# Gated delta net on one NeuronCore: beta moves into the decay scan, key products are multiplied straight from PSUM, query tables take one factor

## What is computed

```python
beta  = sigmoid(x @ W_b.T)                        # per token and value head (32 heads)
decay = exp(-softplus(x @ W_a.T + dt_bias) * exp(A_log))
kk    = kk / max(norm(kk), 1e-12)                 # 16 key heads of 128, 2 value heads for each
def step(state, inp):
    q_t, k_t, v_t, b_t, d_t = inp
    delta = (v_t - k_t . state) * b_t
    state = state * d_t + outer(k_t, delta)
    return state, q_t . state
out = rmsnorm(o) * silu(z);  y = out @ W_out.T
```

## Time and profile before

| | |
|---|---|
| median of 3 runs | 4566.03 us (4562.16 to 4568.08) |
| the profiled execution | 4563.68 us, its span 4561.9 us |
| the 64 sections | from about 135 us to 3100 us of the span |
| PE busy over the span | 88%, VectorE 69%, ACT 49%, POOL 42% |
| granted TensorE clock, mean | 0.957 (1.00 from 500 us to 3000 us) |

### The profile page before, as it was taken

One profiled execution on the slowest core, in us unless ns is written; L12 is line 12 of the kernel. 1 busy time (PEld: TensorE's weight loads), 2 busy tenths in 40 slices (PEclk: granted clock), 3 DMA queues, 4 the chain that ended last, 5 costly groups with the idle time before them and its releaser, 6 DMA issues. The chain is left out here.

```text
span 4561.9 us, 75168 instructions
## 1 busy us (share of the span) xinstructions
PE 4014.6 (88%) x26288; PEld 2924.0 (64%) x26288; DVE 3163.8 (69%) x5082; ACT 2239.2 (49%) x4061; POOL 1893.7 (42%) x1852
## 2 busy tenths in 40 slices
PE   3899999999999999999999999985788879389998
PEld 2677777677777776777767677762344444168887
DVE  3788888888888888888888888874555556532222
ACT  1565656565655556565656565652444445321111
POOL 1364545554554546454555455542233332411110
PEclk8899999999999999999999999996899989689999
DMA  2001010101010101101010101103444553000001
GB/s 74 15 29 35 27 34 20 41 24 32 30 36 25 36 20 32 33 26 35 20 41 24 32 29 34 26 15 69 78 84 77 85 83 59 38 23 19 19 14 37
DMA packets 134066, 172.39 MB, mean 38 GB/s; under 512 B 12524, under 2 KB 79980, under 8 KB 133132
## 3 DMA queue, kind: packets, MB, share of 16 engines
q1 hardware_dynamic: 131212, 166.03, 15.5%
q10 hardware_dynamic: 2432, 1.05, 0.1%
HBM read 143.12 MB, written 21.76 MB: 36 GB/s over the span
## 5 line engine op out<-in xcount | busy, mean ns | idle before, releaser
L405 PE MATMUL pj<-xh,w_hi 128*128 128x512 f32 x1536 | 686.4, 447 | 25.4 <-ACT conv_k L612 16.7
L990 POOL TENSOR_TENSOR silu_z<-silu_z,exp_z 128x512 f32<-128x512 f32 x128 | 184.6, 1442 | 1212.7 <-ACT exp_z L629 1212.7
L405 PE MATMUL pj<-xh,w_lo 128*128 128x512 f32 x1536 | 607.5, 395 | 0.0
L405 PE MATMUL pj<-xl,w_hi 128*128 128x512 f32 x1536 | 602.9, 392 | 0.0
L1510 DVE TENSOR_REDUCE row_max<-s 128x1 f32<-128x512 f32 x512 | 342.0, 685 | 264.4 <-PE s L1264 260.7
L975 POOL TENSOR_SCALAR b_t<-qk_masked,beta_section 128x256 f32<-128x256 f32 (+1 forms) x512 | 490.7, 967 | 20.2 <-ACT qk_masked L714 19.6
L1444 ACT ACTIVATE probs<-s 128x512 f32<-128x512 f32 x512 | 290.6, 595 | 335.8 <-PE s L1288 267.5
L756 DVE SCALAR_TENSOR_TENSOR conv_v<-conv_in,conv_w_section,conv_v 128x512 f32<-128x512 f32 x384 | 402.0, 1047 | 19.4 <-ACT conv_v L612 5.5
L680 ACT ACTIVATE kk_masked<-tp 128x512 f16<-128x512 f32 x320 | 191.3, 598 | 321.8 <-PE tp L496 318.2
L405 PEld LDWEIGHTS pj<-xh,w_hi 128*128 128x128 f32 x1536 | 291.9, 190 | 81.0 <-issue 28.9
L405 PEld LDWEIGHTS pj<-xh,w_lo 128*128 128x128 f32 x1536 | 289.7, 189 | 67.3
(11 more groups left out here) (259 smaller groups left out, 10258.9 us busy)
## 6 DMA issues: line engine op xcount, KB each, us to landing
w_raw<-in_w_in SPq DMA_DIRECT2D x128, 256.0 KB, 3.4
decays<-decay_by_head SPq DMA_DIRECT2D x64, 512.0 KB, 3.8
decays<-decay_by_head SPq DMA_DIRECT2D x64, 256.0 KB, 4.9
q_stack<-qk_parts SPq DMA_DIRECT2D x128, 128.0 KB
k_stack<-qk_parts SPq DMA_DIRECT2D x128, 128.0 KB
f_raw<-in_f_w SPq DMA_DIRECT2D x32, 256.0 KB, 2.6
x_all<-in_x SPq DMA_DIRECT2D x4, 1024.0 KB, 11.2
source<-in_ctx SPq DMA_DIRECT2D x8, 512.0 KB
```

The lines of the kernel that those rows point to most:

```text
L405: mm = pe.matmul(pj[j % 2][:, :], a[:, j, k * P:(k + 1) * P], b[:, k, bp * WIN:(bp + 1) * WIN], start=(n == 0), stop=(n == 3 * KT - 1))
```

## The change

1. `scan_diag` goes. Its place in the scan takes `beta_diag`, a tile of 128 x 4 x 386 with beta of the token on the diagonal, so that the cumulated products come out of the scan already times beta. POOL makes it for the next section (`pool_beta`, two TENSOR_TENSOR of 4 x 128 columns each from the identity and `beta`), behind `pool_b`; `beta_s`, its VectorE copy (L737), goes.
2. `a_t` is made from the PSUM bank of the key product and `decays` (one factor, no copy of the keys by ACT): four instructions of two heads each, in the tail of the section before (`dve_a(t, b, c)`), instead of eight at the section's start.
3. `b_t` is the query product times `decays`: two TENSOR_TENSOR of 4 x 256 and 4 x 128 columns, instead of sixteen instructions. ACT copies only the two query products (`act_queries`).
4. PE makes both key products first (they no longer wait for the query convolution), ahead of the second chunk's first product, and the two query products later. The two projection halves that stood there move down by one place each; the gate's second projection ends one place later.
5. `kk_masked`, whose storage `u_i[0]` and `t_i[0]` used, becomes `t_and_u0`, a tile of its own. Waits follow.

The core of the diff:

```diff
-            dve.tensor_tensor_scan(dec[:, i, :], dec[:, i, :], diag, 0.0, ALU.mult, ALU.add).then_inc(E["dec"].sem, 1)
-        def dve_a(dve, s):
-            E["km"].wait(dve, s, 3)
-            E["beta_s"].wait(dve, s, 0)
-            for q in range(NM):
-                E["dec"].wait(dve, s, q)
-                for c, sl in enumerate((slice(0, SEQ), slice(SEQ, TRI))):
-                    before = dec[:, slot(q), sl.start + c:sl.stop + c]
-                    dve.scalar_tensor_tensor(out=a_t[:, q, sl], in0=kk[:, q // PV, sl],
-                                             scalar=beta_s[:, 2 * (q // PV) + c, q % PV:q % PV + 1], in1=before,
-                                             op0=ALU.mult, op1=ALU.mult).then_inc(E["at"].sem, 1)
-            E["at"].wait(dve, s, 7)
+            dve.tensor_tensor_scan(dec[:, i, :], dec[:, i, :], beta_diag[:, i, :], 0.0, ALU.mult, ALU.add).then_inc(E["dec"].sem, 1)
+        def dve_a(dve, t, b, c):
+            E["kq"].wait(dve, t, b)
+            E["dec"].wait(dve, t, b * PV + PV - 1)
+            sl = (slice(0, SEQ), slice(SEQ, TRI))[c]
+            by_head = dec[:, b:NM:2, sl.start + c:sl.stop + c]
+            dve.tensor_tensor(a_t[:, b * PV:(b + 1) * PV, sl], by_head,
+                              kq_bank[b][:, sl].unsqueeze(1).to_broadcast([P, PV, sl.stop - sl.start]), ALU.mult)\
+               .then_inc(E["at"].sem, 1)
+        def dve_inverse(dve, s):
+            E["at"].wait(dve, s, 3)
...
             E["delta"].wait(pe, s, 0)
             pe_group(pe, up, lambda q: a_t[:, q, P:SEQ], delta[0], "cp")
-            proj(GATE + 1, 0)
-            E["rhs1r"].wait(pe, s, 0)
             E["uc"].wait(pe, s, 1)
-            pe_group(pe, xp[0], lambda q: u_f[:, 1, mat(q)], v_r, "d0p")
-            proj(GATE + 1, 1)
-            E["d0"].wait(pe, s, 1)
-            pe_group(pe, xp[1], lambda q: a_t[:, q, SEQ:TRI], d0[:, :].bitcast(F32), "rp")
             if nxt:
                 pe_kq(pe, s + 1, 0)
                 pe_kq(pe, s + 1, 1)
+            E["rhs1r"].wait(pe, s, 0)
+            pe_group(pe, xp[0], lambda q: u_f[:, 1, mat(q)], v_r, "d0p")
+            proj(GATE + 1, 0)
+            E["d0"].wait(pe, s, 1)
+            pe_group(pe, xp[1], lambda q: a_t[:, q, SEQ:TRI], d0[:, :].bitcast(F32), "rp")
+            proj(GATE + 1, 1)
...
+        def pool_beta(pool, t, hk, bp):
+            if t:
+                E["dec"].wait(pool, t - 1, NM - 1)
+            for c in range(2):
+                o = c * (SEQ + 1) + 1
+                by_head = beta[:, 4 * bp + c:4 * bp + 4:2, hk * PV:(hk + 1) * PV].rearrange("p b h -> p h b")
+                pool.tensor_tensor(beta_diag[:, :, o:o + P].rearrange("p (h b) t -> p h b t", b=2),
+                                   ident.unsqueeze(1).unsqueeze(1).to_broadcast([P, PV, 2, P]),
+                                   by_head.unsqueeze(3).to_broadcast([P, PV, 2, P]), ALU.mult)\
+                    .then_inc(E["bd"].sem, 1)
+
+        def pool_b(pool, s):
+            E["km"].wait(pool, s, 1)
+            E["dec"].wait(pool, s, NM - 1)
             if s:
                 E["op"].wait(pool, s - 1, PV - 1)
+            by_head = dec[:, :, :].rearrange("p (h b) t -> p b h t", b=2)
+            of = b_t[:, :, :].rearrange("p (b h) t -> p b h t", b=2)
             for c, sl in enumerate((slice(0, SEQ), slice(SEQ, TRI))):
...
+                pool.tensor_tensor(of[:, :, :, sl], qk[:, :, sl].unsqueeze(2).to_broadcast([P, 2, PV, sl.stop - sl.start]),
+                                   by_head[:, :, :, sl.start + c + 1:sl.stop + c + 1], ALU.mult).then_inc(E["bt"].sem, 1)
```

106 lines of the change are left out of this document (50 added, 56 removed).

## The result

The changed kernel takes 4648.05 us (median of 4 runs, 4644.32 to 4651.23) against 4566.57 (4 runs) on the same chip: a ratio of 1.018, 95% interval 1.0162 to 1.0197. It is slower by 81.5 us, where 133 were forecast: the sign and the place were right, the sizes too large. The profiled execution has a span of 4648.1 us (before 4561.9).

The account below looks back on a forecast made before the run. PE, busy 88%, was taken to bound the kernel. Ordinary sections 56, first 39, third 35 and prologue 3 sum to 133 us over 4563.7, so 4697, as median 4699; range 4550 to 4745, the forecast's own 4650 to 4745.

Parts of the forecast that it names:

- rival 4: Part of the loss only, 4575 to 4650: ordinary sections lose below 1, first ones 1.5; 4620; chance 0.14.
- signs: What would show it: PE idle over 1 us before first level, first-section inversion 2 us later, longer sections.
- The hold: VectorE instructions with both inputs in SBUF stand until a POOL TENSOR_TENSOR they meet ends; POOL's TENSOR_SCALAR holds nobody.
- Rival 2: Any POOL instruction reading SBUF holds; old holds of some 14 us a section fall to 6.3; 4515; chance 0.03.
- POOL's new list: POOL's four products: long b_t 2.5 us, other three 1.26 each; bounds 1.04 (beta) and 3.2 (long one).
- Where it lies: Section's head: held VectorE work delays the first level's x_l, so PE loses 1.45 us at the first level.
- rival 1: Holds fall less often, shorter VectorE work shows; needs L743's end before +10.6; 4516 to 4550, say 4535; chance 0.16.
- Later in the section: g_lo meets the q convolution, third level's x_l is 0.5 late, some old waits come back; sum +0.1.
- The tail: Between cp group and second d0p, PE has 1.31 us of key products instead of 1.44 of projection; costs 0.2.
- First section: First section of a head (15): four VectorE instructions each held behind one of POOL's four; +2.6, 39 us.
- Third section: 16 with weight splits, which now also hold the first v convolution: about 1.1 less 0.7; +2.2, 35 us.
- Prologue: A memset and two beta products ahead of the first weight split, partly under its DMA; +3.

Follow-up runs that it names:

- e1: The changed kernel with POOL's beta products moved behind the last convolution tap; 4553.39 us, ratio 0.9971 to the kernel before.
- e2: The changed kernel with the beta products made by eight TENSOR_SCALARs, not two TENSOR_TENSORs, in the old place; 4563.41 us, ratio 0.9996 to the kernel before.
- e8: The kernel before the change with POOL's first factor of b_t by TENSOR_TENSOR instead of TENSOR_SCALAR; 4706.14 us, ratio 1.0304.
- e7: The changed kernel with POOL's b_t and beta products as sixteen short TENSOR_TENSORs, not four long ones, same place; 4575.35 us, ratio 1.0015 to the kernel before.
- e6: The e5 kernel with POOL's g_lo waiting for the last tap of the q convolution; 4468.84 us, ratio 0.9785 to the kernel before.
- e3: The changed kernel with the tail's old order on PE and VectorE's first a_t block behind the residual; 4707.73 us, ratio 1.0317 to the kernel before.
- e10: The kernel before the change with the waits, splits and loads of e6, its b_t still sixteen instructions; 5008.64 us, ratio 1.0968.
- e4: The changed kernel with b_t and beta products behind the last convolution tap, four weight loads ahead of a head's last decays; 4639.58 us, ratio 1.0158.
- e5: The e4 kernel with first-section products ahead of the output-weight splits, two of a head's splits moved to the fourth section; 4522.27 us, ratio 0.9901.

## Why the prediction was right, by its steps

The time, 4648, lies in the stated range (4550 to 4745), but 2 us below the 4650 where the forecast's own part of it begins: by size it was rival 4, given a chance of 0.14, that came about, by the forecast's mechanism. Two of the signs came smaller than named: PE's wait before the first level was 0.91 and not over 1, and its start of the inversion in a first section came 0.73 later for the first half (1.59 for the second), not 2. The three kinds of section took 46.1, 49.0 (third) and 49.8 (first), not 47, 49.5 and 51. And PE's idle time in the earlier trace rows begins at 2.1 us (45.23 less 43.14), not 2.2.

- **The hold.** Right, and shown: VectorE ends 0.55 (0.28 for the halves of U) after POOL's TENSOR_TENSOR in the rows above; e1 takes two of POOL's away and VectorE's lengths go back to 0.68; e2 and e8 show from both sides that a TENSOR_SCALAR of POOL doesn't hold; e7 shows the alternation. Rival 2 (the rule's reading) falls by e2 and e8. The prediction had left out the CAST, which holds as well (e2), and that the TENSOR_SCALAR itself stands for VectorE (1.31 instead of 0.60). So the sentence at the start of this document that the engines meet only at semaphores is too narrow: these two meet at SBUF as well. That an input in PSUM frees VectorE agrees with all rows (L806 at 0.74) and was not tried by itself.
- **POOL's new list.** Sizes too large. Forecast 2.5 for the long b_t, 1.26 for the others; where nobody meets them they take 2.19 and 1.18 (b_t) and 1.04 (beta), in e6. The beta products are at the lower bound that the text named (1.04).
- **Where it lies.** The order came out as written, instruction by instruction. What failed is the sum of its times: the four POOL instructions took from +4.35 to +10.54, not +4.5 to +11.3, so L738 ended at +11.2 instead of +12.1 and PE's first level came at +11.55 instead of +12.45. A loss of 0.55 where 1.45 stood; this term, 32 times over, is the largest error, 29 us. The deciding point of rival 1 (L738 ending before +10.6) was missed by half a microsecond. PE also wanted U earlier than the forecast had it: it starts the inversion at +6.60 and +7.07 and waits 0.07, so the 0.30 was won after all, only to be waited for at the first level.
- **Later in the section.** Forecast +0.1 net. PE's starts show 0.08, from +0.55 to +0.63, as a larger loss at the third level (0.77 of waiting, not 0.5) and a larger recovery ahead of the output projection.
- **The tail.** Forecast +0.2, measured 0.1 (0.63 to 0.73). The old order, in e3, saves nothing at full clock and loses some 60 us with the clock.
- **First section.** Forecast +2.6, measured +1.15 (1.3 without the two of the kernel before that had a clock of 0.97). All four holds are there; each of POOL's instructions was priced too high, so the second half of the inversion starts at +10.7 instead of +11.5.
- **Third section.** Forecast +2.2 for 16 with weight splits; 15 have them and lose 3.1, the one term that was too small. The earlier splits now meet the v convolution in two places (1.15 and 1.76) where the forecast had one new stall of 1.1 and 0.7 given back. Some 6 us of the 47 come from three sections in which the clock fell (below). This term being too small hides 12 us of what the others had too much.
- **Prologue.** Forecast +3, measured +0.6.

With the ordinary section at +0.78 this is what rival 4 described (ordinary below 1, first ones about 1.5), except for the third sections, which bring the time from that rival's 4620 up to the end of its range, 4650.

## What to carry to other kernels

When work moves between engines, ask of each instruction on POOL what VectorE runs beside it, and compare VectorE's length of the same instruction before and after: a busy share that rises while the instruction count falls is the sign. Cutting POOL's work by a quarter made this kernel 1.8% slower, and the same work 20 us later in the section, with g_lo and the weight splits moved too, made it 2.1% faster than the kernel before; here the fewer and longer TENSOR_TENSORs were a gain only where VectorE had PSUM inputs or nothing to do. Then follow what the late work releases: here a buffer, the load behind it and a scan set a deadline (about +30 of a section). Missing it by 5 us in every section cost 443 us (e10), more than all the holds; missing it in the first sections alone cost 117 (e4 against e5). And where waits stand close together, read the granted clock behind them as well: it may have fallen (e3).

## What the runs showed of the hardware that was not expected

**The clock can fall after a cluster of waits.** The third section of the first head of the changed kernel took 52.85 us instead of 49. Stretches of it, clock in the last number but two:

```profile
226.32:250.00 23.68, 21.88 (x172) 16.27 (x170) 22.57 (x27) 16.77 (x32) 17.05 (x12) 1.00 0.22 67
250.00:260.00 10.00, 7.10 (x61) 4.86 (x60) 7.92 (x11) 3.21 (x6) 5.03 (x5) 0.91 0.10 28
260.00:270.00 10.00, 9.08 (x44) 7.12 (x44) 4.37 (x8) 3.03 (x5) 0.00 (x0) 0.58 0.00 0
```

PE was idle 2.9 of 10 us, and then, although busy 9.1 of the next 10, was granted 0.58, so mostly the lower level (1.2 instead of 2.4 GHz). The same two waits (1.16 and 1.74) stand in all 15 third sections that have weight splits, and 12 of these keep 1.00, as do all second and fourth ones; in e3, where 0.99 and 0.79 ahead of the inversion stand in place of the 0.91 of the first level, one of the 15 keeps it. It is not the change that brought this in: two first sections of the kernel before, behind waits of 0.8 and 1.2, stood at 0.97 (49.6 us instead of 48.2 to 48.5). A stall can thus cost twice, once as idle time and once, in some sections, as 1.2 to 5.4 us at the lower level. What decides between two sections with the same waits was not found, and no run changed the clock alone. In the stretch of e10 above, PE is busy 2.2 of 8.2 us, and the clock is 0.80. The forecast priced idle time alone; in the changed kernel that was nearly enough (6 us), in e3 (67 us) and e7 (22 us) it was not.

**POOL's TENSOR_SCALAR is the slower and the quieter one.** Where nobody meets it, one of 128x128 takes 0.60 (e2), a TENSOR_TENSOR of that size 0.41 (L982 in e10). In e2 eight of them take 6.38 us, 0.80 each, against 4.25 for eight TENSOR_TENSORs of the same size in e7 (0.53 each, with VectorE in their way); and yet the kernel is no slower for it (ratios 0.9996 and 1.0015 to before, with intervals that overlap).
